# Gated cross-attention and spiking feed-forward block: a new order of the work ahead of the batch loop, query and key offsets as extra moving columns, and a new tail

## The reference

```python
# per batch; latents = layernorm(x) without gain; gm, bm, gl, bl are 512 wide
xn = layernorm(ctx, gm, bm); ln = layernorm(latents, gl, bl)
q = ln @ Wq
k, v = split(concat([xn, ln]) @ Wkv)            # 974 keys
attn = softmax(8 * q @ k.T)                     # per head
x = x + tanh(g_xattn) * (attn @ v) @ Wout
y = square(relu(layernorm(x) @ W_fc.T)) @ W_proj.T
# five leaky integrate-and-fire steps on y, spikes counted, / 5
x = x + tanh(g_ffn) * spikes
```

## Time and profile before

| | |
|---|---|
| median of 3 runs | 1082.3 us (1081.94 to 1082.74) |
| the profiled execution's own time | 1082.14 us |
| its span, first to last instruction | 1080.3 us |
| PE busy | 1054.5 us, 98% |
| DVE, ACT, POOL busy | 744.9, 590.6, 296.2 us |
| chain that ended last | PE 95%, DVE 3%, POOL 1%, ACT 1% |

### The profile page before, as it was taken

One profiled execution on the slowest core, in us unless ns is written; L12 is line 12 of the kernel. 1 busy time (PEld: TensorE's weight loads), 2 busy tenths in 40 slices (PEclk: granted clock), 3 DMA queues, 4 the chain that ended last, 5 costly groups with the idle time before them and its releaser, 6 DMA issues.

```text
span 1080.3 us, 19327 instructions
## 1 busy us (share of the span) xinstructions
PE 1054.5 (98%) x7105; PEld 865.8 (80%) x7105; DVE 744.9 (69%) x1164; ACT 590.6 (55%) x1125; POOL 296.2 (27%) x270
## 2 busy tenths in 40 slices
PE   4999999999999999999999999999999999999996
PEld 4888878877878887887787788788788888998885
DVE  6567777877867777787786777759534555585765
ACT  5547647555745764755574576457445433445535
POOL 3024435324444343532444434343000000000000
PEclk9999999999999999999999999999999999999998
DMA  7201000201201100020120200013431000201011
GB/s 221 101 1 49 28 19 16 73 0 34 74 0 34 51 23 25 10 73 0 34 74 0 73 0 0 26 32 105 144 113 44 1 1 26 92 1 43 17 59 40
DMA packets 31511, 47.43 MB, mean 44 GB/s; under 512 B 2416, under 2 KB 10624, under 8 KB 31472
## 3 DMA queue, kind: packets, MB, share of 16 engines
q1 hardware_dynamic: 31132, 46.39, 13.1%
q10 hardware_dynamic: 340, 0.52, 0.2%
HBM read 39.56 MB, written 7.34 MB: 43 GB/s over the span
## 4 chain that ended last, share of the span: by engine, by line
PE 95%; DVE 3%; POOL 1%; ACT 1%; issue 0%; DMA 0%; SPq 0%; DVEq 0%; POOLq 0%
PE work L438 41%; PE work L606 13%; PE score L619 13%; PE heads_out L558 9%; PE score L521 9%; PE score L453 2%; PE maxes L543 1%; PE maxes L533 1%; PE heads_out L570 1%; PE score L799 1%; PE heads_out L438 1%; DMA xin<-in_ctx 0%; POOL xin L1804 0%; DVE on L1358 0%; DVE xT L1386 0%
## 5 line engine op out<-in xcount | busy, mean ns | idle before, releaser
L1758 POOL TENSOR_TENSOR dsum<-dsum,probs 125x448 f32<-125x448 f32 x186 | 226.8, 1219 | 14.6
L438 PE MATMUL work<-wv,xT 128*125 128x512 f32 (+1 forms) x768 | 187.2, 397 | 0.0
L438 PE MATMUL work<-xT,wk 128*128 128x488 f32 (+1 forms) x768 | 185.6, 392 | 0.6 <-DVE xT L1386 0.6
L438 PEld LDWEIGHTS work<-wv,xT 128*125 128x125 f32 (+1 forms) x768 | 137.7, 183 | 36.6 <-issue 2.3
L438 PEld LDWEIGHTS work<-xT,wk 128*128 128x128 f32 x768 | 140.3, 188 | 31.5 <-issue 4.6
L606 PE MATMUL work<-zT,wf 128*128 128x512 f32 (+1 forms) x768 | 164.0, 364 | 0.5 <-DVE wf L1417 0.5
L920 ACT ACTIVATE probs<-score 125x448 f32<-125x448 f32 (+1 forms) x256 | 120.0, 549 | 70.1 <-PE score L521 69.6
L1755 POOL TENSOR_TENSOR dsum<-probs 125x448 f32<-125x448 f32 x31 | 35.8, 1156 | 425.9 <-ACT probs L926 425.9
L606 PEld LDWEIGHTS work<-zT,wf 128*128 128x128 f32 x768 | 131.5, 189 | 23.1 <-issue 0.9
L1311 DVE TENSOR_TENSOR probs<-probs,maxes 125x1792 f32<-125x1792 f32 x64 | 128.2, 2013 | 5.8 <-PE maxes L543 5.1
L619 PE MATMUL score<-hT,wp 128*128 128x512 f32 (+1 forms) x576 | 117.5, 354 | 0.1
(11 more groups left out here) (181 smaller groups left out, 1416.1 us busy)
## 6 DMA issues: line engine op xcount, KB each, us to landing
xin<-in_ctx SPq DMA_DIRECT2D x42, 250.0 KB
neuron<-in_L_ffn_W_fc SPq DMA_DIRECT2D x16, 256.0 KB, 3.8
neuron<-in_L_ffn_W_proj SPq DMA_DIRECT2D x16, 256.0 KB, 2.8
xres<-in_x SPq DMA_DIRECT2D x16, 224.0 KB, 2.6
x_scratch<-xres SPq DMA_DIRECT2D x16, 224.0 KB, 2.5
out<-fin SPq DMA_DIRECT2D x14, 256.0 KB, 2.1
xin<-in_x SPq DMA_DIRECT2D x14, 224.0 KB, 9.6
zt<-x_scratch SPq DMA_DIRECT2D x3, 1024.0 KB, 6.5
```

Source lines behind the costliest of these rows:

```text
L438: mm = pe.matmul(bank, lhs(i, k), rhs(j, k), start=(n == 0), stop=(n == len(passes) * chunks - 1))
L1758: pool.tensor_tensor(total[0:ROWS[t]], total[0:ROWS[t]], tile(t), ALU.add).then_inc(dchain if t < TILES - 1 else dsum_done, 1)
```

## The change

**Offsets of keys and queries.** xT gets two columns more at each end (`XO = 2`): at either end stand bm and bl themselves. The key product (c, 0) and the query product (c, 2) take these two as moving columns, once for each c: in the head for (0,0), (1,0), (0,2), (1,2), (2,0), in every batch for (2,2), (3,0), (3,2). ACT copies the two resulting columns into `shift` before it makes the hi part. The row products, rows and transposed columns of keys and queries are gone; that of the values stays.

**Head.** Loads: SP tiles 0, 2, the first half of the key weights, tiles 4, 6, the query weights; ACT the vectors, tiles 1, 3, the second half of the key weights, tiles 5, 7. Statistics, variances (now on DVE) and roots go by pairs of tiles. ACT normalises tiles 0, 2, 5, 7 and POOL 1, 3, 4, 6. POOL makes the low part of one quarter of the key weights and of all value and output weights. PE runs 32 transposes of the identity between tiles 3 and 4. Products go in the order (0,0), (1,0), (0,1), (0,2), (1,1), (1,2), (2,0), (2,1).

**Tail.** `unit_back(2)` moves into the second `last_down`, after matmuls of j = 11. DVE runs units 3 and 4 without a break and finishes units 2 and 3 behind them. The last group is stored in four transfers: three column blocks of two tiles each after unit 2, the fourth block of tiles 0 and 1 after unit 3, of tiles 2 and 3 after unit 4.

```diff
-        xT = sb(a, "xT", [P, 2, DC, KEYS], F32R)
+        xT = sb(a, "xT", [P, 2, DC, KEYS + 2 * XO], F32R)
+        FIRST = [(0, 0), (1, 0), (0, 1), (0, 2), (1, 1), (1, 2), (2, 0), (2, 1)]
+        FIRST_SHIFTS = [(0, 0), (1, 0), (0, 2), (1, 2), (2, 0)]
+        LATE_SHIFTS = [(2, 2), (3, 0), (3, 2)]
+        LN_ACT = (0, 2, 5, 7)
+        LN_POOL = (1, 3, 4, 6)
...
 SP:
-            for t in range(2):
+            for t in (0, 2):
                 first_tile(t)
-            load_weight(0, Wkv[:, 0:D], staged[0])
-            for t in range(4, TILES):
+            sp.dma_start(staged[0][:, 0:2, :],
+                         Wkv[0:2 * P, 0:D].rearrange("(k p) n -> p k n", p=P)).then_inc(wk_in[0], 16)
+            for t in (4, 6):
                 first_tile(t)
...
+            def store_units():
+                cut = (DC - 1) * P
+                rows = group_rows(out_flat, FINAL)
+                sp.wait_ge(fin_done, T0[FINAL] + DC - 1)
+                for i in range(2):
+                    two = slice(2 * i, 2 * i + 2)
+                    sp.dma_start(rows[:, two, 0:cut], fin[:, two, 0:cut]).then_inc(fin_out, 16)
+                for i in range(2):
+                    two = slice(2 * i, 2 * i + 2)
+                    sp.wait_ge(fin_done, T0[FINAL] + DC + i)
+                    sp.dma_start(rows[:, two, cut:D], fin[:, two, cut:D]).then_inc(fin_out, 16)
...
 PE:
+                    ends = XO if with_shift(c, u, first) else 0
+                    lo, hi = ((XO - ends, XO + HALF), (XO + HALF, XO + KEYS), (XO + T, XO + KEYS + ends))[u]
+                    product(bank[:, 0:hi - lo], lambda i, k: (wk if u < 2 else wq)[:, i, k, cols],
+                            lambda i, k: xT[:, i, k, lo:hi], DC).then_inc(kq_mm, 1)
...
+            def warm(n):
+                for i in range(n):
+                    pe.transpose(maxes[:, i % DC * P:(i % DC + 1) * P], ident[:, :], ident[:, :])
...
-            first_transposes(0)
+            first_transposes(0, 1, 2, 3)
+            warm(32)
             pe.wait_ge(w_lo[0], DC)
-            pe.wait_ge(shift_lo, 1)
-            pe.wait_ge(gain_ready, 1)
-            row_product(wk, LT, k_row_mm)
-            first_transposes(1)
-            row_columns(k_row, k_shift_mm)
-            keys_queries(0, 0, (0, 1), first=True)
+            first_transposes(4, 5, 6, 7)
+            keys_queries(0, 0, (0,), first=True)
+            keys_queries(0, 1, (0,), first=True)
+            keys_queries(0, 0, (1,), first=True)
             pe.wait_ge(w_lo[1], DC)
-            row_product(wq, LT, q_row_mm)
-            keys_queries(0, 0, (2,))
-            row_columns(q_row, q_shift_mm)
-            keys_queries(0, 1, (0,))
+            keys_queries(0, 0, (2,), first=True)
+            keys_queries(0, 1, (1,), first=True)
+            pe.wait_ge(kq_done, 4)
             scores(0, 0, 0, first=True)
-            keys_queries(0, 1, (1,))
+            keys_queries(0, 1, (2,), first=True)
+            keys_queries(0, 2, (0,), first=True)
             scores(0, 0, 1)
-            keys_queries(0, 1, (2,))
-            keys_queries(0, 2, (0, 1))
+            keys_queries(0, 2, (1,), first=True)
...
-                last_down(0, TG // 2, 3, 1)
-                last_down(TG // 2, TG // 2, 0)
-                unit_back(2)
+                last_down(0, TG // 2, 3, back=1, after=6)
+                last_down(TG // 2, TG // 2, 0, back=2, after=11)
                 unit_back(3)
                 unit_back(4)
...
 ACT:
+                    if ends:
+                        done = first_shift if first else late_shift
+                        n = FIRST_SHIFTS.index((c, u)) + 1 if first else b * 3 + (LATE_SHIFTS.index((c, u)) + 1)
+                        at = 0 if u == 0 else L
+                        act.activation(shift[:, u // 2, c, :], bank[:, at:at + ends], ACT.Copy).then_inc(done, 1)
+                        act.wait_ge(done, n)
...
+            first_norm(0)
+            split_hi(0, wk, 0, 1)
+            first_norm(2)
+            split_hi(0, wk, 2, 3)
             hi_chunks(0, 0, 0, 1, 2, 3)
+            first_norm(5)
+            first_norm(7)
+            split_hi(1, wq, 0, 1)
             hi_chunks(0, 1, 0, 1, 2, 3)
             kq_hi_parts(0, 0, 0, first=True)
+            split_hi(1, wq, 2, 3)
+            kq_hi_parts(0, 1, 0, first=True)
...
+            kq_hi_parts(0, 0, 1, 2, first=True)
+            split_hi(2, wv, 0, 1, 2, 3)
+            kq_hi_parts(0, 1, 1, first=True)
             act.wait_ge(pad_ready, 1)
             copy_scores(0, 0, 0, 1, first=True)
+            kq_hi_parts(0, 1, 2, first=True)
             copy_scores(0, 0, 2, 3, first=True)
+            kq_hi_parts(0, 2, 0, first=True)
+            split_hi(3, wo, 0, 1, 2, 3)
+            kq_hi_parts(0, 2, 1, first=True)
             take_row(v_row_mm, v_row)
...
 DVE:
+            first_statistics(0)
+            first_statistics(1)
+            split_lo(0, wk, 0, 1)
+            first_statistics(2)
+            split_lo(0, wk, 2)
+            first_statistics(3)
             lo_chunks(0, 0)
+            split_lo(1, wq, 0, 1)
             lo_chunks(0, 1)
+            kq_lo_parts(0, 0, 0, first=True)
+            split_lo(1, wq, 2, 3)
+            kq_lo_parts(0, 1, 0, first=True)
...
-                unit_steps(3, 0, 4)
+                unit_steps(3, 0, 9)
                 finish_unit(2)
-                unit_steps(3, 4, 9)
-                unit_steps(4, 0, 4)
+                unit_steps(4, 0, 9)
                 finish_unit(3)
-                unit_steps(4, 4, 9)
                 finish_unit(4)
...
 POOL:
+            first_root_of(0)
+            first_norm(1)
+            first_root_of(1)
+            first_norm(3)
+            split_lo(0, wk, 3)
+            first_root_of(2)
+            first_root_of(3)
+            first_norm(4)
+            first_norm(6)
+            split_lo(2, wv, 0, 1, 2, 3)
+            split_lo(3, wo, 0, 1, 2, 3)
             with pool.Fori(0, NA - 1) as b:
                 batch(b, False)
```

More of the change, by code:

```diff
@@ L225, in flamingo_block @@
         w_lo = [sem(f"w_lo{i}") for i in range(4)]
+        wk_in = [sem(f"wk_in{i}") for i in range(2)]
         pad_ready = sem("pad_ready")
+        first_ve = sem("first_ve")
+        first_root = sem("first_root")
+        first_rstd = sem("first_rstd")
+        ln_act = sem("ln_act")
+        ln_pool = sem("ln_pool")
+        ends_hi = sem("ends_hi")
+        first_shift = sem("first_shift")
+        late_shift = sem("late_shift")
         x_in = [sem(f"x_in{i}") for i in range(TILES)]
@@ L463, in keys_queries @@
                         pe.wait_ge(xlo_done, b * 2 * DC + (4, 8)[u])
-                    n = 3 * c + u
+                    n = kq_index(c, u, first)
                     if n == 8:
@@ L497, in values @@
                     pe.wait_ge(kq_done, b * 12 + 9)
[L498 removed]
+                product(value_bank(t)[0:ROWS[t], :], lambda i, k: xT[:, i, k, XO + AT[t]:XO + AT[t] + ROWS[t]],
                         lambda i, k: wv[:, i, k, :], DC).then_inc(v_mm, 1)
@@ L726, in row_columns, with first_transposes @@
                 mm.then_inc(done, 1)
-            def first_transposes(g):
-                for t in range(4 * g, 4 * g + 4):
-                    pe.wait_ge(ln_done, t + 1)
+            def first_transposes(*ts):
+                for t in ts:
+                    g = t // 4
+                    if t in LN_ACT:
+                        pe.wait_ge(ln_act, LN_ACT.index(t) + 1)
+                    else:
+                        pe.wait_ge(ln_pool, LN_POOL.index(t) + 1)
                     at = AT[t] - GROUP_AT[g]
@@ L790, in group_transposes, with last_down @@
                     group_transpose(g, i)
-            def last_down(at, n, bank, back=None):
+            def last_down(at, n, bank, back, after):
                 if bank == 0:
@@ L803, in last_down @@
                         mm.then_inc(y_mm, 1)
-                    if j == 6 and back is not None:
+                    if j == after:
                         unit_back(back)
@@ L931, in kq_hi_parts @@
                 s = c % 2
-                if not first:
+                if not first or c == 2:
                     act.wait_ge(s_mm, b * PAIRS * STEPS_S + (c - 1) * STEPS_S)
                 for u in us:
-                    act.wait_ge(kq_mm, b * 12 + (3 * c + u + 1))
-                    bank = kq_bank(c, u)
+                    act.wait_ge(kq_mm, b * 12 + (kq_index(c, u, first) + 1))
+                    bank = kq_bank(c, u, first)
+                    ends = XO if with_shift(c, u, first) else 0
+                    if ends:
[4 more added lines that the diff above has]
+                        act.wait_ge(done, n)
                     if u == 0:
-                        act.activation(kst[:, s, 0, 0:HALF], bank[:, 0:HALF], ACT.Identity,
+                        act.activation(kst[:, s, 0, 0:HALF], bank[:, ends:ends + HALF], ACT.Identity,
```

(31 more changed lines are left out.)

157 lines of the change are left out of this document (71 added, 86 removed).

## The result

| | before | changed |
|---|---|---|
| median | 1082.26 us, 4 runs | 1073.57 us, 4 runs (1072.93 to 1074.86) |
| profiled execution, its span | 1082.14, 1080.3 | 1072.93, 1071.1 |
| PE busy, ACT busy, POOL busy | 1054.5, 590.6, 296.2 | 1049.2, 593.2, 306.9 |

The account below looks back on a forecast made before the run. PE bounds the kernel from 28 to 1066 us, so other gains lie in head and tail. Head -6.6, loop and columns +0.3, tail -3.5 sum to -9.8: 1072.3 us, median 1072.5, range 1070.4 to 1078.6.

Parts of the forecast that it names:

- When the first key product starts: Head: loads, roots, normalisations and transposes let it start at 21.5, so the value row product at 44.3; head -6.6 us.
- two issuing queues of equal halves end no later: Head loads: same bytes, traffic before faded in 15 to 16 us, so splitting the issue costs no time.
- I keep 6.9 for it: Head loads: tile 1, issued about 0.4 us later but sharing with less, still lands at 6.9; bounds 6 to 8.
- PE's work from there: Head, first key product to value row product: 22.6 us plus a 0.15 stall before (1,1), taken as 22.8.
- Warm transposes: Head: 32 transposes on PE from 14.2 take 3.7 to 7.2 us, taken as 5.3, ending at 19.6.
- Rival A: Head: the transposes don't bring the clock up; head only -1.0, time 1078.1 us; chance 0.25.
- Covers: Head: POOL's low parts of value and output weights and SP's later loads stay hidden; at worst 0.5 us, taken as nothing.
- Loop: Loop: ACT's 24 shift copies stay hidden and the extra columns cost 0.35 us; +0.3, bounds 0 to +2.
- Rival C: PE reads of shifted, wider xT rows get slower, 10 ns on each of 1536 matmuls; 15 us, 1087.9 us; chance 0.04.
- D: Loop: PE waits for the shift copies; 6 us, time 1078.5 us; chance 0.03.
- Tail: After the last matmuls: moved back product, units run without a break, smaller last store; -3.5 us, bounds -2.3 to -4.1.
- Rival B: Head: something is late, ACT's ten transfers or POOL held by DVE; costs 3.3 us, time 1075.8 us; chance 0.08.

Follow-up runs that it names:

- e8: Changed kernel with all head loads issued as in the kernel before; 1070.90 us median, ratio 0.9896.
- e12: Kernel before with only the changed kernel's issue of the head's loads; 1085.98 us median, ratio 1.0036.
- e6: Changed kernel with a 12-matmul product the size of the removed query row product put back, result unused; 1075.46 us median.
- e1: Changed kernel with the whole tail of before (back product, order of finishing units, stores); 1077.48 us median.
- e13: Changed kernel, loads still split over two queues, but the four vectors issued behind tiles 1 and 3 on ScalarE's queue; 1073.60 us median.
- e5: Changed kernel without the loop's late offsets (no extra columns or ScalarE copies for three key products), part of the biases left out; 1072.58 us, timed once.
- e9: Kernel before with xT's rows 978 elements apart in place of 974, nothing else; 1081.45 us, timed once.
- e2: Changed kernel with only the last group's stores as before (whole tiles, two after unit 3, two after unit 4); 1075.22 us median.
- e4: Changed kernel with the query weights' load held back until tiles 5 and 7 have landed; 1073.12 us median.
- e10: Changed kernel with loads issued as before, except that ScalarE issues the four vectors ahead of tiles 2 and 3; 1072.74 us median.
- e3: Changed kernel with the 32 transposes of the identity taken out; 1074.83 us median.

## Why the prediction was right, and where not

The sum held, 9.8 forecast against 8.7 by the medians and 9.2 in the profile. That it came so near is partly luck: the head was forecast 2.2 us too large, and a gain in the loop that had no term (0.9) and a tail whose last product happened to find the clock up (0.5) made up for part of it.

- **When the first key product starts.** The step that failed is "two issuing queues of equal halves end no later" and with it "I keep 6.9 for it". Tile 1 was issued 0.65 us later than before (from 2.33 for 1.68), not 0.4. Tiles 1, 3 and 5 landed at 7.6, 10.6 and 15.9. What is behind came later: second root 13.4 for 11.6, fourth 20.65 for 18.0, POOL's tile 6 22.16 for 20.7, first key product 23.53 for 21.5. With the loads of before (e8) it is 21.49, so the loads were mis-sized by 2.0 us; e12 shows their price from the other side, +3.7. That e8 meets 21.5 to the digit is luck too, for the path behind the loads was wrong. The forecast ran over POOL's roots and tile 6. In e8 the fourth root with its shift ends at 18.6 for 18.0 and tile 6 at 20.11 for 20.6 to 20.9, but the chain runs over DVE, busy for 8.53 of the 8.67 us from 11.47 to 20.14, whose low part of the first four tiles was forecast to end at 19.3. PE waits for that, and 13 transposes stand behind it where two tiles' eight were forecast. How much of the head's gain the pairs and the work shared with POOL give by themselves, no run shows.
- **PE's work from there.** 22.82 us measured (46.35 - 23.53), 22.8 forecast. The forecast took the start at 24.40 from the timeline and the end at 50.86 from the chain; in the timeline the value row product starts at 50.70, which makes the forecast 22.6 and the value row product's start 44.1, and leaves the -6.6 as it was. The stall in front of (1,1) was 0.46 and not 0.15, which is more than the 0.2 that the measured is over; the matmuls gave back 0.1.
- **Warm transposes.** 4.37 us for 32, within 3.7 to 7.2; in the nine profiles that have 32 it is 3.66 (e6) to 5.25 (e1). Rival A fell. Between 14.32 and 20.4 PE did nothing but transposes, and all 32 took 4.37 us, where the lower level's 0.22 each would make 7. The count of matmuls that touch each us shows the rise (columns as above).

```profile
16.00:17.00 1.00, 1.00 (x7) 1.00 (x6) 0.93 (x5) 1.00 (x3) 0.67 (x1) 1.00 0.79 209
17.00:18.00 1.00, 1.00 (x9) 1.00 (x8) 1.00 (x4) 1.00 (x2) 0.72 (x1) 1.00 0.06 23
18.00:19.00 1.00, 1.00 (x12) 1.00 (x10) 0.99 (x2) 0.47 (x2) 0.55 (x2) 1.00 0.28 14
```

  The Trainium skill (TensorE: Matmul & The Clock Gate, Part 4: PE-mode transpose) has it that a transpose doesn't count as busy for the clock in the way a matmul does. For the float32 transposes here this trace doesn't agree, and the measurement decides. In e6 the 32 ran at 0.114 each from their start, PE then idled 2.23 us, and the 13 transposes behind took 2.77 us in place of 1.52; e13 shows the same after 1.76 us. So the level can be lost again before the products, where it was kept over the 1.09 us of the changed kernel.
- **Covers.** POOL's low parts of value and output weights held up nobody, and neither did the late loads on SP: PE idles 1.7 us from 28 to 1063 us, 0.46 of it in front of (1,1), where the prediction allowed 2.
- **Loop.** +0.3 forecast, -0.64 measured. The columns cost 0.04 a batch (e5), the copies nothing. The term left out is how fast PE's matmuls go by where xT's rows lie: -0.08 a batch by their spacing (e9) and -0.06 that stays open, so -0.10 net. Rival C had that mechanism with the other sign, and D fell. C's count of 1536 matmuls is short: 1152 stream xT and 768 hold it as weights, 1920 in all.
- **Tail.** -3.5 forecast, -4.2 measured: 3.7 by the edit (e1, e2) and 0.5 by the clock. Unit 4's first step came 0.44 after the last matmul, for 0.4, and its nine steps took 3.98 us, for 3.95. Stores 0.9 for 0.7.
- **Rival B** (something of the head is late, ACT's ten transfers ahead of its first pass, POOL held by DVE) is the nearest to what came: 2.2 us of the 3.3 that it named, by the landings and not by ACT's issuing.

## What to carry to other kernels

Where every engine waits for the first bytes, the order of issue is part of the critical path, and byte counts don't price it: read when each tile landed, from the wait of the instruction that takes it, and keep an order whose landings the trace shows to be good, while all around it is changed. Undoing the loads alone was the best edit here (e8, 1070.9 us, 11.4 below before). Split a term whose parts rest on one another, as head start and PE's work do, and check each against the trace: a sum that comes out right can hold two errors, and so can a single time on the way to it.

## What the runs showed of the hardware that I had not expected

- Four transfers of 2 KB issued ahead of tiles on ACT's queue: 100 to 220 GB/s between 3 and 4 us in nine executions against 344 to 387 in three with the order of before, and tile 3 landed at 10.3 to 11.7 against 9.0 or before (before, e8).
- A DVE step on 2 columns took 1.18 us (e4) and 1.13 (e10) beside POOL's operation on 512 columns with two inputs, and POOL's root of two columns 0.70 alone, 1.30 in e1, 1.90 in e3 beside DVE's split of the key weights. It looks as if each of the two engines can hold the other; in e4 the two operations end together, at 17.00 and 17.02.
- Rows of 3912 bytes in place of 3896 make twelve matmuls of 486 columns 0.08 us faster (2.91 for 2.99), those of 488 columns not (e9).
- TensorE's clock differs between executions of one kernel at the same idle stretch: after 3.9 us of idleness the last back product found it at the upper level three times and at the lower seven times.
